# Expert outputs scattered by index to their tokens' rows in the expert stage, so that the mixing stage loads plain blocks

## The reference, cut to what matters

```python
cum = jnp.cumsum(onehot, axis=0) - 1            # place of a (token, k) pair within its expert
keep = loc < C                                  # C = ceil(K * S / E * 1.25) = 1280
gates = top_vals * keep; gates = gates / max(gates.sum(-1), 1e-9)
buf = zeros((E, C + 1, h)).at[e_flat, l_flat].set(xk)     # rows sorted by expert
hid = einsum('ech,ehf->ecf', buf[:, :C], W_in)
a, g = split(hid, 2); hid = gelu(a) * g
out_e = einsum('ecf,efh->ech', hid, W_out)
gathered = concat([out_e, zeros])[e_flat, l_flat]         # back to the order of tokens
y = (gathered * gates[..., None]).sum(axis=1)             # two rows per token
x = x + attention(xn) + y
```

## Time and profile before

| | |
|---|---|
| median of three runs | 2156.84 us |
| the profiled execution | 2144.84 us, span 2143.1 us |
| PE busy over the span | 1966.0 us (92%) |
| DVE, ACT, POOL busy | 1531.1 (71%), 1035.6 (48%), 514.3 us (24%) |
| expert stage, PE busy in 1066 to 1443 us | 366.47 of 377 us |
| mixing stage, PE busy in 1443 to 1570 us | 78.92 of 127 us |

### The profile page before, as it was taken

The page is one execution under the profiler, slowest core; times in us unless marked ns, Lnnn a source line. Parts: engine busy times, 40 slices in busy tenths (PEclk is TensorE's granted clock), DMA queues, the critical chain, the costliest instruction groups (busy, mean ns, idle before and its releaser), DMA issues. The chain is left out here.

```text
span 2143.1 us, 35073 instructions
## 1 busy us (share of the span) xinstructions
PE 1966.0 (92%) x11874; PEld 1195.0 (56%) x11874; DVE 1531.1 (71%) x3473; ACT 1035.6 (48%) x2246; POOL 514.3 (24%) x932
## 2 busy tenths in 40 slices
PE   6869999999999999999799999986678999999998
PEld 3333333333333333333299999984556777777776
DVE  7879988888888888888054333325578998889883
ACT  3426677676767777777744444432331122221112
POOL 4554123322222222222233333336400000000000
PEclk9979999999999999999999999998789999999998
DMA  6555111111101111110133222215410000000005
GB/s 206 183 160 200 62 38 58 56 38 40 35 32 38 41 43 43 43 43 11 52 101 100 90 84 88 90 42 163 144 51 12 9 21 20 20 20 20 10 11 162
DMA packets 111781, 143.69 MB, mean 67 GB/s; under 512 B 12153, under 2 KB 96769, under 8 KB 111233
## 3 DMA queue, kind: packets, MB, share of 16 engines
q1 hardware_dynamic: 87248, 98.09, 14.3%
q0 software_dynamic: 10400, 31.47, 4.4%
q10 hardware_dynamic: 13968, 12.06, 1.8%
HBM read 85.10 MB, written 56.10 MB: 66 GB/s over the span
## 5 line engine op out<-in xcount | busy, mean ns | idle before, releaser
L854 ACT ACTIVATE at_wt<-at_B 128x512 f32<-128x512 f32 (+3 forms) x1280 | 607.3, 538 | 257.7 <-PE at_B L953 240.8
L1259 DVE TENSOR_REDUCE at_piece_max<-at_A 128x1 f32<-128x512 f32 x768 | 489.0, 684 | 71.3 <-PE at_A L934 61.8
L971 PE MATMUL at_O<-at_wt,at_v 128*32 128x512 f32 (+3 forms) x2560 | 313.9, 543 | 0.0
L754 POOL TENSOR_SCALAR_AFFINE_SELECT at_wt<-at_wt 128x128 f32<-128x128 f32 x512 | 147.8, 294 | 632.6 <-ACT at_wt L854 623.9
L1256 DVE CUSTOM_DVE_ANT_0 at_junk<-at_A,s_hide 128x128 bf16<-128x128 f32 (+3 forms) x512 | 230.5, 487 | 69.6 <-PE at_A L934 69.0
L1474 PE MATMUL ex_H<-ex_xT,ex_w_in 128*128 128x256 f32 x1920 | 247.8, 286 | 4.0 <-DVE ex_xT L1581 4.0
L1474 PEld LDWEIGHTS ex_H<-ex_xT,ex_w_in 128*128 128x128 f32 x1920 | 237.0, 193 | 4.4 <-DVE ex_w_out L1586 4.4
L1595 DVE TENSOR_TENSOR ex_h<-ex_act_a,ex_H 128x256 f32<-128x256 f32 x160 | 66.8, 417 | 212.7 <-ACT ex_act_a L1523 212.6
L2170 ACT ACTIVATE l_act_g<-l_G 128x512 f32<-128x512 f32 x80 | 47.9, 599 | 305.9 <-PE l_G L2084 241.3
L934 PE MATMUL at_A<-s_k,s_q 96*128 96x512 bf16 (+2 forms) x480 | 165.7, 363 | 22.3 <-PEq L104 9.6
L1516 POOL TENSOR_TENSOR ex_hT<-ex_h,ex_hT 128x256 fp32r<-128x256 f32 x160 | 123.1, 774 | 254.3 <-ACT ex_hT L1527 254.3
(11 more groups left out here) (275 smaller groups left out, 2798.9 us busy)
## 6 DMA issues: line engine op xcount, KB each, us to landing
buf<-at_room POOLq DMA_DIRECT2D x10, 1024.0 KB, 8.7
s_first_rows<-buf SPq DMA_DIRECT2D x40, 256.0 KB, 2.7
expert_out<-ex_y ACTq DMA_DIRECT2D x40, 256.0 KB, 2.2
s_raw_in<-in_W_in SPq DMA_DIRECT2D x8, 1024.0 KB
q_parts<-parts SPq DMA_DIRECT2D x16, 384.0 KB, 3.5
s_down<-in_x SPq DMA_DIRECT2D x8, 512.0 KB, 4.7
xn<-s_raw_in SPq DMA_DIRECT2D x8, 512.0 KB, 5.4
at_v<-v SPq DMA_DIRECT2D x16, 256.0 KB, 3.0
```

The source lines that it names most:

```text
L754: pool.affine_select(block_, block_, [[1, P]], ALU.is_ge, 0.0, base=0, channel_multiplier=-1).then_inc(hidden, 1)
L854: act.activation(wt[(HP * p + h) % NE_][:, q0:CH], pB_of(p, h, u)[:, q0:CH], ACT.Exp, scale=D ** -0.5).then_inc(wt_ready, 1)
L971: pe.matmul(pO[j % 2][rows, q0:CH], vs[n % 3][:, kt // TPC, kt % TPC, :], wt[(HP * p + h) % NE_][:, q0:CH], start=kt < 2 and not late, sto ...
L1259: ins = dve.tensor_reduce(top, pA[slot % NA][:, 0:w], AX.X, ALU.max)
```

## The change

The rows that go to the experts grow from 256 to 258 floats: in front stands the token's number, behind the number of the token's second expert. `zeros` carries a far-off number in front, so that an empty slot names no row. In the expert stage DVE works out for each of a block's rows the row of `expert_out` to which it belongs: the token, plus 4096 if this expert is the token's second one (`find_target`). POOL writes the outputs there with two indirect transfers for each block, one behind the low part of f=1 and one behind that of f=2 of the next block. ACT stores nothing there any more. `expert_out` has 8192 rows now, in the order of tokens, first experts and then second ones; POOL zeroes it with eight transfers of 1 MB in the attention's second pair of heads. The mixing stage has no POOL work: SP loads the two blocks of expert rows with plain transfers behind `x`. The loops of SP, POOL and DVE in the expert stage are written out; some semaphores of layer 1 are shared.

```diff
             def dispatch(n):
                 pool.wait_ge(xrow_in[n % 2], 32 * (n // 2 + 1))
+                if n == 0:
+                    pool.wait_ge(routing_in, 48)
+                    pool.tensor_copy(token[:, :, 1], expert[:, 1]).then_inc(token_set, 1)
+                    pool.wait_ge(token_set, 2)
+                if n >= 2:
+                    pool.wait_ge(put[n % 2], 16 * 2 * TOPK * (n // 2))
                 for w in range(2):
-                    for c in (2 * n + w, TILES + 2 * n + w):
+                    pool.tensor_copy(xrow[n % 2][w][:, 0:E + 2:E + 1], token[:, 2 * n + w]).then_inc(token_set, 1)
...
+                    if n == 1 and p % 4 == 0 and p // 4 < NO_ROWS:
+                        pool.dma_start(no_rows[p // 4],
+                                       zeros[:, 1:E + 1].unsqueeze(1).to_broadcast([P, 8, E])).then_inc(buf_blank, 16)
...
@@ experts, POOL
-            with pool.Fori(0, ROUNDS) as j:
-                for i in range(PAIR):
-                    for f in range(FC):
-                        pool.wait_ge(h_high, FC * (PAIR * j + i) + f + 1)
-                        pool.tensor_tensor(hT[i % 2][1][:, f, :], h[i % 2][:, f, :],
-                                           hT[i % 2][0][:, f, :].bitcast(F32), ALU.subtract).then_inc(h_low, 1)
+            def store(m, t):
+                if t == 0:
+                    pool.wait_ge(target_ready, 2 * (m + 1))
+                    pool.wait_ge(y_ready, m + 1)
+                pool.indirect_dma_start(
+                    out=d["expert_out"], out_offset=bass.IndirectOffsetOnAxis(ap=target[m % 8][:, t:t + 1], axis=0),
+                    in_=y[m % 2][:, t, :], in_offset=None, bounds_check=TOPK * NT - 1, oob_is_err=False,
+                ).then_inc(y_stored[m % 2], 16)
+
+            for m in range(PAIR * ROUNDS):
+                for f in range(FC):
+                    pool.wait_ge(h_high, FC * m + f + 1)
+                    pool.tensor_tensor(hT[m % 2][1][:, f, :], h[m % 2][:, f, :],
+                                       hT[m % 2][0][:, f, :].bitcast(F32), ALU.subtract).then_inc(h_low, 1)
+                    if f in STORE_AT and m:
+                        store(m - 1, STORE_AT.index(f))
+            for t in range(RT):
+                store(PAIR * ROUNDS - 1, t)
+            for i in range(2):
+                pool.wait_ge(y_stored[i], 16 * RT * (PAIR // 2 * ROUNDS))
...
@@ experts, ACT
-            def store(m, i):
-                act.wait_ge(y_ready, m + 1)
-                act.dma_start(one(rows_out, m), y[i][:]).then_inc(y_stored[i], 16)
...
@@ experts, DVE
+            def find_target(m, u):
+                dve.wait_ge(x_loaded[u % 2], 16 * (m // 2 + 1))
+                wait(dve, y_stored[u % 2], 16 * RT * (m // 2 - 3))
+                dve.tensor_scalar(second[u][:], x[u % 2][:, :, E + 1], float(m // PER), float(NT), ALU.is_equal,
+                                  ALU.mult).then_inc(target_ready, 1)
+                dve.wait_ge(target_ready, 2 * m + 1)
+                dve.tensor_tensor(target[u][:], second[u][:], x[u % 2][:, :, 0], ALU.add).then_inc(target_ready, 1)
...
+                        if f == 1 and not (last and i == PAIR - 1):
+                            find_target(m + 1, (m + 1) % 8)
...
@@ mixing, SP
             def load(t):
                 wait(sp, sums, SUMS * (t - NR) + 1)
                 sp.dma_start(x[t % NR][:], x_rows[t]).then_inc(x_in[t % NR], 16)
+                wait(sp, sums, SUMS * (t - NR + 1))
+                for k in range(TOPK):
+                    sp.dma_start(ye[k][t % NR][:], ye_rows[k][t]).then_inc(rows_in[t % NR], 16)
...
@@ mixing, POOL
-                        pool.indirect_dma_start(
-                            out=ye[k][t % NR][:, w, :], out_offset=None, in_=d["expert_out"],
-                            in_offset=bass.IndirectOffsetOnAxis(ap=s["slot_get"][:, c:c + 1], axis=0),
-                        ).then_inc(rows_in[t % NR], 16)
```

More of the change, by code:

```diff
@@ L41 @@
 SLOTS = NX * CAP
+FAR = float(1 << 20)
 NPAT = 32
@@ L506, in attention @@
         raw = [sb(f"raw{i}", [P, CH]) for i in range(2)]
-        xrow = [[sb(f"xrow{i}{k}", [P, E]) for k in range(2)] for i in range(2)]
+        xrow = [[sb(f"xrow{i}{k}", [P, E + 2]) for k in range(2)] for i in range(2)]
         KT = TOPK * TILES
@@ L533, in attention @@
         tile_count, tile_before = (scratch(KT * NX) for _ in range(2))
-        loc, within, drop, slot, slot_low, slot_put, kept = (scratch(KT) for _ in range(7))
-        FAR = float(1 << 20)
+        loc, within, drop, slot, slot_put, kept = (scratch(KT) for _ in range(6))
         def half(i):
@@ L1371, in experts @@
         y = [sb(f"y{i}", [P, RT, E]) for i in range(2)]
+        second = [sb(f"second{i}", [P, RT]) for i in range(8)]
+        target = [sb(f"target{i}", [P, RT], U32) for i in range(8)]
         over_sum = sb("over_sum", [P, TILES, H])
@@ L1414, in pieces @@
             return found
+        STORE_AT = (1, 2)
         CUTS = len(pieces(0))
@@ L1452, in round_ @@
                         weights(2 * j + i // PER + 1)
-            with sp.Fori(0, ROUNDS - 1) as j:
-                round_(j, True)
-            round_(ROUNDS - 1, False)
+            for j in range(ROUNDS):
+                round_(j, j + 1 < ROUNDS)
         @block.tensor
@@ L1558, in round_ @@
                             keep(m - 1, 1 - b)
-                        if f == 2 and not (first and i == 0):
-                            store(m - 1, 1 - b)
                         if f == 2:
@@ L1572, in _ @@
             keep(PAIR * ROUNDS - 1, 1)
-            store(PAIR * ROUNDS - 1, 1)
-            for i in range(2):
-                act.wait_ge(y_stored[i], 16 * (PAIR // 2 * ROUNDS))
         @block.vector
@@ L1619, in _ @@
             xT_rest(0, 0)
-            round_(0, True, False)
-            with dve.Fori(1, ROUNDS - 1) as j:
-                round_(j, False, False)
-            round_(ROUNDS - 1, False, True)
+            find_target(0, 0)
+            for j in range(ROUNDS):
+                round_(j, j == 0, j == ROUNDS - 1)
 def mixing(nc, d, s):
@@ L1705, in _ @@
                 sp.wait_ge(x1_out[u], 16 * ((STEPS - 1 - u) // NR + 1))
-        @block.gpsimd
-        def _(pool):
-            for t in range(STEPS):
-                wait(pool, sums, SUMS * (t - NR + 1))
-                for k in range(TOPK):
-                    for w in range(2):
-                        c = k * TILES + 2 * t + w
-                        pool.indirect_dma_start(
-                            out=ye[k][t % NR][:, w, :], out_offset=None, in_=d["expert_out"],
-                            in_offset=bass.IndirectOffsetOnAxis(ap=s["slot_get"][:, c:c + 1], axis=0),
-                        ).then_inc(rows_in[t % NR], 16)
         @block.tensor
```

60 lines of the change are left out of this document (34 added, 26 removed).

## The result

The changed kernel took 2173.84 us (median of 20 runs, 2164.64 to 2180.31), the kernel before 2158.03 (20 runs, 2145.35 to 2169.75) in the same comparison: ratio 1.0078, 95% interval 1.0064 to 1.0092. The profiled execution took 2180.31 us, that of before 2144.84: 35.5 us apart where the medians are 15.8 apart.

What follows compares the result with a forecast made beforehand. The prediction took PE to bound the experts and short steps with holes to bound mixing. Experts +54, barrier +2.4, mixing -30 and attention +1 gave +27 on 2150.84: 2178 us, range 2120 to 2206.

Steps and rivals of the forecast that it cites:

- base of 2150.84: Whole kernel: starting time for the sum, halfway between the profiled execution (2144.84 us), 12 us below the median, and that median.
- Experts, +54: Expert stage: two scatters at 1.48 us each delay POOL's last low part, period 9.06 to 10.44 us, +54 us.
- period of 10.02: Expert stage, lower bound: at 1.27 us for each scatter the period of an output is 10.02 us, +38 us.
- the same sum holds with cuts: Expert stage: blocks in which DVE cuts weights pay the same 1.38 us as the others.
- Barrier, +2.4, at most 4: End of the expert stage: issue and landing of the last two scatters, 4.6 against 2.2 us, +2.4, between 1 and 4.
- Mixing, -30: Mixing stage: holes go with the gathers, 14 steps at 4.57 us, 33 us less, 3 taken off for late blocks.
- Attention, +1: Attention's second pair of heads: eight more zeroing transfers of 1 MB, +1 us, between 0 and 8.
- A: Rival, expert stage: scatters do not hold POOL's later subtractions, only mixing counts, -27 us, 2124 us; chance 0.22.
- C: Rival, mixing: the holes stay, coming from traffic or PE and not the gathers, +52 us, 2203 us; chance 0.10.
- B: Rival: a scatter costs 1.27 us and mixing gives all of 33 us, +8 us, 2159 us; chance 0.13.
- D: Rival, expert stage: a DVE cut holds up one scatter in 21 blocks, 0.74 us each, 16 us more, 2194 us; chance 0.10.

Runs made afterwards that it cites:

- s33: Changed kernel with both scatters of a block behind POOL's fourth low part instead of the second and third: 2107.35 us, 1.0049 of the kernel before.
- best2: best1 with the last block's two rows by index written by POOL in the mixing stage: 2094.52 us, 0.9985 of the kernel before; again in III: 2108.91 us, 0.9783.
- I: First comparison, changed kernel against the kernel before: 2173.84 against 2158.03 us, ratio 1.0078.
- plain_mix_2: Kernel before with plain loads in mixing (rows added are not those of its tokens), run again in III: 2116.19 us, 0.9827 of the kernel before.
- II: Second comparison of the same two kernels, unchanged, on another chip: changed kernel 2148.81 us, kernel before 2097.77 us, ratio 1.0240.
- best1: Changed kernel with both scatters behind the fourth low part and buf filled in pieces of 1024 bytes: 2103.22 us, 1.0023 of the kernel before.
- s00: Changed kernel with both scatters of a block behind POOL's first low part: 2122.7 us, 1.0121 of the kernel before.
- III: Later comparison of variants with the unchanged kernel before, on another chip: kernel before 2156.7 us.

## Why the prediction was right, and where it was not

The forecast was 2178 us for 2173.84, and the mechanism is the one named. That the number is so near is luck. The sum was +27 us on a base of 2150.84; the medians are 15.8 us apart on a base of 2158.03, and the two profiles 35.5 us. Of the terms one is near in size and three are off, and they partly cancel.

- **Experts, +54:** measured +45.7 (T to T, 39 periods). The order on POOL and the path were right. Mis-sized was the scatter's gap: I took 1.48 us from a scatter behind a mask in the earlier trace rows, and it was 1.17. The period of 10.02 that I gave as the lower bound is that of the blocks without cuts (10.01). That "the same sum holds with cuts" was wrong: they have 10.29, since a scatter beside a cut takes longer. s33, with period 9.05, shows that nothing but the place costs.
- **Barrier, +2.4, at most 4:** failed. I worked out issue and landing, both of which came true, and left out POOL's drain, which went from 0.78 to 6.6 us. best2, which takes it and the two scatters off the path, is 8.7 us faster. About 2 us more of the +11.3 are the last `output` at the lower clock. The trace of the kernel before had such a drain already, at the end of the attention (`--source L475`):
```profile
L475 POOLq DRAIN  x1: 7773/7773/7773, 1060.8 to 1060.8; - x1
```
POOL had issued 106 transfers in that stage, 64 of them by index, the last of them 27 us earlier (its issue ends at 1033.96), and PE waits 5.7 us for this drain. It is the row from which the term could have been priced.
- **Mixing, -30:** -33.9 in I, just over the bound of 33. Plain loads cost DVE no wait that can be seen. The reason, holes that go with the gathers, is shown by plain_mix_2. That these holes are not in each comparison, only hinted at in my choice of the base, is the larger lesson: in II the same term is -4, and the change costs 2.4%. My range of 2120 to 2206 rests on one base; relative to the kernel before, II (1.0240) lies just above its upper end (2206 of 2156.84, 1.023).
- **Attention, +1:** +10.9 in I, +6.3 in II up to the first `output`. I priced the eight transfers to `expert_out`, which cost nothing in II, and took the wider rows for 0.8% more bytes, in the scatters. I gave no price to the fill of `buf`, whose rows of 1032 bytes take 1.3 to 1.6 times as long to land. Another 2.7 and 3.8 us lie ahead of the first pair. No run isolates them, and best1 and best2, which are alike up to there, begin that pair at 175.3 and 170.7 us, so they may be no more than the spread of single executions.
- **Base:** the execution profiled was 13 us under the median of comparison I, that of the changed kernel 6.5 over. This alone makes the profiles 20 us further apart than the medians.

Of the rivals, A (scatters hold nothing back) falls with the timeline, C (holes stay) with plain_mix_2. B's price of a scatter, 1.27 us, was nearer than mine. D is right in its mechanism and too high in its price: one of the two scatters is held up in each of the 21 blocks with cuts, but by 0.27 us and not 0.74, so it adds 6 us (21 x 0.28) and not 16. With that the stage comes out: 39 x (10.01 - 9.05) = 37 us for the places, 6 for the cuts, and about 2 for the first blocks with their divisions, which is the 45.7 measured. That DVE holds the scatter is read from its end, always 0.26 to 0.27 us behind the cut's in the changed kernel and 0.24 to 0.25 in s00; no run moves the cuts alone.

Open: what delays PE's updates in mixing by 2.5 to 11 us. From the first to the last sum of mixing the granted clock was 0.80 in I and 0.78 in III, against 0.93 in II and 0.96 with plain loads in III. But the holes themselves idle PE, so the low clock can be their effect as well as their cause. Gathers are needed for it and do not suffice. The three later sets ran on three chips, so a difference between chips is a rival that no run here excludes.

## What to carry to other kernels

Ask of an engine not whether it has time, but at which point of its order: two scatters behind the last wanted instruction cost the period nothing, the same two ahead of it 46 us. Look too at what DVE does beside a scatter, since a cut beside it made it up to 0.4 us longer. Transfers that POOL issues in a stage cost a drain at its end, even 27 us after the last of them, so let POOL's part of the stage end before the other engines' last work, or put its last scatters into the next stage. The DRAIN stands in the trace, in the view of its line. Where the gain is the removal of waits that the profile lays to nobody, expect it to be there in one comparison and gone in the next: profile the kernel before more than once.

## What the runs showed of the hardware

- POOL's DRAIN at the end of a stage ended 0.07 us behind POOL's last computing instruction where POOL had issued no transfer in the stage, and took 0.21 us with two by index, 6.59 us with 80 and 6.95 with 78, though all had landed. With 106, 64 of them by index, it took 7.77 us (the attention of the kernel before). Whether the number is what sets it was not tested.
- A scatter of 128 rows by index took 0.98 to 1.00 us on POOL, and 1.26 to 1.27 us (1.37 to 1.49 in s00) beside a subtraction of DVE that cuts weights. POOL's next instruction started only behind it, in each of the 80 cases.
- A fill in rows of 1032 bytes landed in 12.0 to 14.1 us, in pieces of 1024 bytes in 8.7 to 9.4. A packet of four such rows, 4128 bytes, took 283 ns on the mean and one of 4096 bytes 173 ns in the first pair of heads of comparison I, and 241 and 170 ns in II.
- After 3.98 us without work on PE the clock granted in its next 24 matmuls was 0.55 on the mean, and they took 5.24 us; after 2.25 us (s33) it was 1.00, and they took 3.14.
- The same kernel took 2098 us in two comparisons and 2157 in two others, with updates from PE to ACT up to 11 us late in mixing and most later pairs of heads 0.7 to 3.7 us longer in the slower ones.
